# The order of the work in the first pair of sequences: copies, weight splits, finishes and sums change places

## The reference

```python
w1, w2 = W1[language_ids], W2[language_ids]              # layer 0: an adapter, 512 -> 128 -> 512
h = relu(x @ w1 + b1[language_ids])
y = x + h @ w2 + b2[language_ids]
x = x + layernorm(y) * gamma[language_ids] + beta[language_ids]
h = gelu(x @ W1m + b1m)                                  # layer 1: 512 -> 2048, shared weights
x = x + concat([h @ W2m + b2m,                           # 384 shared output columns
                h @ We[indices] + be[indices]], -1)      # 128 columns of the sequence's own expert
```

## Time and profile before

| | |
|---|---|
| median of 3 runs | 1474.71 us (1471.84 to 1479.5) |
| profiled execution | 1473.23 us, its span 1471.4 us |
| PE busy | 1449.9 us (99%) |
| DVE, POOL, ACT busy | 939.9, 649.4, 524.6 us |
| mean granted TensorE clock | 0.996 |

### The profile page before, as it was taken

How to read it: one execution, slowest core, us unless ns; L and a number is a source line. 1 busy time by engine, 2 the same in 40 slices (tenths; PEclk the granted TensorE clock), 3 DMA queues, 4 the chain that set the end, 5 groups by cost and what they waited for, 6 DMA issues and landing times.

```text
span 1471.4 us, 19128 instructions
## 1 busy us (share of the span) xinstructions
PE 1449.9 (99%) x6454; PEld 1189.2 (81%) x6454; DVE 939.9 (64%) x1597; ACT 524.6 (36%) x855; POOL 649.4 (44%) x639
## 2 busy tenths in 40 slices
PE   8989999999999999999999999999999999999999
PEld 5777778888887888888888888888888888888887
DVE  6878775766648666576566775666755776554444
ACT  4724353332533225322344322523234332342231
POOL 4795544623445334545246351483413843242101
PEclk9999999999999999999999999999999999999999
DMA  6655558444655536655356554456446464354332
GB/s 212 209 170 185 216 194 294 157 150 168 211 204 175 167 128 236 220 162 196 126 173 222 173 188 147 174 209 204 144 157 225 148 215 154 113 214 145 140 109 87
DMA packets 126617, 261.98 MB, mean 178 GB/s; under 512 B 11573, under 2 KB 83765, under 8 KB 118457
## 3 DMA queue, kind: packets, MB, share of 16 engines
q1 hardware_dynamic: 116724, 156.68, 33.3%
q10 hardware_dynamic: 9796, 104.08, 18.1%
HBM read 222.98 MB, written 37.75 MB: 177 GB/s over the span
## 4 chain that ended last, share of the span: by engine, by line
PE 90%; DVE 4%; POOL 3%; issue 2%; ACT 1%; ACTq 1%; DVEq 0%; POOLq 0%
PE down L251 15%; PE down L253 15%; PE down L252 15%; PE up_b L251 5%; PE up_b L253 5%; PE up_b L252 5%; PE up_c L251 4%; PE up_c L252 3%; PE up_c L253 3%; PE up_a L252 3%; PE up_a L253 3%; PE up_a L251 3%; DVE g L872 1%; PE aux L251 1%; PE aux L253 1%
## 5 line engine op out<-in xcount | busy, mean ns | idle before, releaser
L251 PE MATMUL down<-w,g 128*128 128x512 f32 x1024 | 401.6, 392 | 0.9 <-issue 0.5
L253 PE MATMUL down<-w,g 128*128 128x512 f32 x1024 | 398.9, 390 | 0.0
L252 PE MATMUL down<-w,g 128*128 128x512 f32 x1024 | 398.9, 390 | 0.0
L1198 POOL TENSOR_TENSOR w<-w_raw,ones 128x256 fp32r<-128x256 f32 x128 | 90.2, 704 | 633.9 <-DMA w_raw<-m_we 633.8
L251 PEld LDWEIGHTS down<-w,g 128*128 128x128 f32 x1024 | 192.5, 188 | 42.1 <-DVE g L872 1.9
L253 PEld LDWEIGHTS down<-w,g 128*128 128x128 f32 x1024 | 192.5, 188 | 40.5
L252 PEld LDWEIGHTS down<-w,g 128*128 128x128 f32 x1024 | 192.6, 188 | 39.4
L872 DVE TENSOR_TENSOR g<-g_raw,g 128x512 fp32r<-128x512 f32 x256 | 205.3, 818 | 22.9 <-ACT g L660 20.6
L658 ACT ACTIVATE g_raw<-up_a,m_b_sb 128x512 f32<-128x512 f32 x64 | 44.2, 690 | 413.7 <-PE up_a L253 386.0
L867 DVE TENSOR_TENSOR g_raw<-up_b,s 128x512 f32<-128x512 f32 x63 | 43.5, 691 | 225.0 <-PE up_b L253 180.9
L660 ACT CAST g<-g_raw 128x512 fp32r<-128x512 f32 x256 | 159.1, 621 | 8.1
(11 more groups left out here) (246 smaller groups left out, 2508.6 us busy)
## 6 DMA issues: line engine op xcount, KB each, us to landing
w<-w_kept ACTq DMA_DIRECT2D x55, 1792.0 KB, 7.6
w<-w_kept SPq DMA_DIRECT2D x56, 768.0 KB, 4.9
w_raw<-m_we SPq DMA_DIRECT2D x128, 128.0 KB, 4.6
out<-resid SPq DMA_DIRECT2D x64, 256.0 KB, 4.5
xTs_raw<-xT SPq DMA_DIRECT2D x56, 256.0 KB, 3.1
xs<-x SPq DMA_DIRECT2D x56, 256.0 KB, 4.6
w_kept<-w SPq DMA_DIRECT2D x8, 1792.0 KB, 8.0
aw_raw<-a_w SPq DMA_DIRECT2D x30, 256.0 KB, 4.5
```

Of the source, the lines that this page charges most:

```text
L251: eng.matmul(bank, a_hi, b_hi, start=opens, stop=False, skip_group_check=True)
L252: eng.matmul(bank, a_hi, b_lo, start=False, stop=False, skip_group_check=True)
L253: return eng.matmul(bank, a_lo, b_hi, start=False, stop=closes, skip_group_check=True)
L1198: eng.tensor_tensor(hi, values, ones[:, :, :].to_broadcast([P, 2, PART]), ALU.mult).then_inc(pool_eh[b], 1)
```

## The change

Only the order of instructions in the first pair and the split of one weight operation change. No product and no transfer is added or removed.

```diff
 pe_p1, second pair, k == 0:
-            eng.wait_ge(act_w1hi, GROUPS)
+            eng.wait_ge(pool_w1, 4)
             eng.wait_ge(dve_w1, GROUPS)
 act_second_step:
         act_g(eng, i, 1, C11)
-        act_w1_hi(eng, 2)
-        act_t_hi(eng, i, T4, 0)
-        act_t_hi(eng, i, T4, 1)
         act_xT_hi(eng, m, 0, 2)
         act_xT_hi(eng, m, 0, 3)
         act_aw_hi(eng, m, 0, 1)
+        act_t_hi(eng, i, T4, 0)
+        act_t_hi(eng, i, T4, 1)
         act_g(eng, i, 1, C12)
+        act_w1_hi(eng, 2)
         act_g(eng, i, 1, C22)
 act_step, last group, next pair's T1:
-            act_t_hi(eng, m, T1, 1)
-        act_g(eng, i, k, C22)
+            if i is not first:
+                act_t_hi(eng, m, T1, 1)
+        act_g(eng, i, k, C22)
+        if i is first and k == GROUPS - 1:
+            act_t_hi(eng, m, T1, 1)
 new:
+    def dve_finishes(eng, m, k):
+        if m and k - 1 in ADAPTER_DOWN:
+            b, t = ADAPTER_DOWN[k - 1]
+            dve_finish(eng, m, b, t)
+            dve_finish(eng, m, b, t + 1)
-    def dve_second_w1_lo(eng):
+    def dve_rest_w1_lo(eng, k):
+        eng.wait_ge(act_w1hi, k)
+        eng.tensor_tensor(w1[:, k % 2, LO, A22:7, :], w1_raw[:, k % 2, LO, A22:7, :], raw(w1[:, k % 2, HI, A22:7, :]),
                           ALU.subtract).then_inc(dve_w1, 1)
 dve_second_step:
         dve_sum_c22(eng, i, 1)
+        dve_xT_lo(eng, m, 0, 2)
+        dve_xT_lo(eng, m, 0, 3)
         dve_g_lo(eng, i, 0, C12)
         dve_g_lo(eng, i, 0, C22)
         dve_w2_lo(eng, 1)
         dve_g_lo(eng, i, 1, C11)
-        dve_xT_lo(eng, m, 0, 2)
-        dve_xT_lo(eng, m, 0, 3)
         dve_w1_lo(eng, 2)
 dve_step:
         elif i is not first:
-            dve_sum_c21(eng, before(i), GROUPS - 1)
+            if before(i) is not first:
+                dve_sum_c21(eng, before(i), GROUPS - 1)
...
             dve_sum_u2(eng, i, k)
-        if m and k - 1 in ADAPTER_DOWN:
-            (the two dve_finish)
+        if i is not first:
+            dve_finishes(eng, m, k)
...
         dve_sum_c22(eng, i, k)
         dve_g_lo(eng, i, k, C11)
+        if i is first:
+            dve_finishes(eng, m, k)
         (the two dve_add_adapter)
-        if i is first:
+        if i is first and k < GROUPS - 1:
             dve_w1_lo(eng, k + 1)
+        if i is first and k == GROUPS - 1:
+            dve_rest_w1_lo(eng, GROUPS)
+            dve_g_lo(eng, i, k, C12)
...
         if k == GROUPS - 1:
-            dve_g_lo(eng, i, k, C12)
+            if i is first:
+                dve_sum_c21(eng, i, k)
+            else:
+                dve_g_lo(eng, i, k, C12)
             dve_g_lo(eng, i, k, C22)
 pool_first_w1_lo: n == 3 does w1 slot 0, columns A11 to S4 (768), after act_w1hi 8
 pool_first_step:
-        if k == 2:
-            pool_aw_lo(eng, m, 1, 0)
         pool_weight_sums(eng, k + 1)
         if k == 1: (T4 low parts, experts, aw, the four pool_residual of sequence 0)
+            pool_aw_lo(eng, m, 1, 0)
         if k == GROUPS - 1:
-            for of, c in t_order(m)[:4]:
+            for n, (of, c) in enumerate(t_order(m)[:4]):
                 pool_t_lo(eng, m, of, c)
+                if n == 0:
+                    pool_first_w1_lo(eng, 3)
 start, PE: B21's first transpose goes right behind B11's two; each low pass of B21 behind its own
            transpose; C21 = A21 x B11 behind the B22 transposes
 start, ACT:
-            act_w1_hi(eng, 1)
+            act_first_part(eng, B11, 0, FIRST_B11[0])
             act_first_x_copy(eng, 3)
-            (first parts of B11, both c)
+            act_first_part(eng, B11, 1, FIRST_B11[1])
+            act_first_part(eng, B21, 0, FIRST_B21[0])
             (low parts of B11, both c)
-            (first parts of B21, both c)
+            act_w1_hi(eng, 1)
+            act_first_part(eng, B21, 1, FIRST_B21[1])
             (low parts of B21, both c)
```

More of the change, by code:

```diff
@@ L999, in dve_first_t4 @@
         eng.tensor_tensor(bo_raw[:, T4, c, LO, :], b21_raw(c), t2_raw(c), ALU.subtract).then_inc(dve_t, 1)
-    def dve_second_w1_lo(eng):
-        eng.wait_ge(act_w1hi, 1)
-        eng.tensor_tensor(w1[:, 1, LO, A22:7, :], w1_raw[:, 1, LO, A22:7, :], raw(w1[:, 1, HI, A22:7, :]),
+    def dve_rest_w1_lo(eng, k):
+        eng.wait_ge(act_w1hi, k)
+        eng.tensor_tensor(w1[:, k % 2, LO, A22:7, :], w1_raw[:, k % 2, LO, A22:7, :], raw(w1[:, k % 2, HI, A22:7, :]),
                           ALU.subtract).then_inc(dve_w1, 1)
@@ L1110, in dve_step @@
             dve_sum_u2(eng, i, k)
-        if m and k - 1 in ADAPTER_DOWN:
-            b, t = ADAPTER_DOWN[k - 1]
-            dve_finish(eng, m, b, t)
-            dve_finish(eng, m, b, t + 1)
+        if i is not first:
+            dve_finishes(eng, m, k)
         if m and k == 1:
@@ L1175, in pool_first_w1_lo @@
         else:
-            slot, s = 1, slice(A11, A22)
-            eng.wait_ge(act_w1hi, 1)
+            slot, s = 3 - n, slice(A11, A22)
+            eng.wait_ge(act_w1hi, 1 if n == 2 else GROUPS)
         eng.tensor_tensor(w1[:, slot, LO, s, :], w1_raw[:, slot, LO, s, :], raw(w1[:, slot, HI, s, :]),
@@ L1388, in keep_w1 @@
         eng.wait_ge(dve_w1, k)
-        if k == 1:
-            eng.wait_ge(pool_w1, 3)
+        if k in (1, GROUPS):
+            eng.wait_ge(pool_w1, 3 if k == 1 else 4)
         eng.dma_start(raw(w1_kept[k % GROUPS, :, :, :, :]), raw(w1[:, k % 2, :, :, :])).then_inc(kept_w1[k % 2], 16)
@@ L1573, in _ @@
                         pe_first_transpose(eng, B11, c, FIRST_B11[c])
+                    pe_first_transpose(eng, B21, 0, FIRST_B21[0])
                 if t == 2:
@@ L1576, in _ @@
                         pe_first_low(eng, B11, c, FIRST_B11[c])
-            pe_first_transpose(eng, B21, 0, FIRST_B21[0])
             pe_first_b12(eng, 0)
@@ L1580, in _ @@
             pe_first_transpose(eng, B21, 1, FIRST_B21[1])
+            pe_first_low(eng, B21, 0, FIRST_B21[0])
             eng.wait_ge(pool_w1, 2)
@@ L1583, in _ @@
             pe_first_b12(eng, 1)
-            for c in range(2):
-                pe_first_low(eng, B21, c, FIRST_B21[c])
+            pe_first_low(eng, B21, 1, FIRST_B21[1])
             pe_first_b12(eng, 2)
-            first_half(eng, C21, A21, B11, True, False)
             pe_first_b12(eng, 3)
@@ L1590, in _ @@
                 pe_transpose(eng, first, 1, 2 + c, FIRST_B22[c])
+            first_half(eng, C21, A21, B11, True, False)
             eng.wait_ge(b_low, 4)
@@ L1624, in _ @@
                 act_first_x_copy(eng, t)
-            act_w1_hi(eng, 1)
+            act_first_part(eng, B11, 0, FIRST_B11[0])
             act_first_x_copy(eng, 3)
-            for c in range(2):
-                act_first_part(eng, B11, c, FIRST_B11[c])
+            act_first_part(eng, B11, 1, FIRST_B11[1])
+            act_first_part(eng, B21, 0, FIRST_B21[0])
             for c in range(2):
                 act_first_low(eng, B11, c, FIRST_B11[c])
-            for c in range(2):
-                act_first_part(eng, B21, c, FIRST_B21[c])
+            act_w1_hi(eng, 1)
+            act_first_part(eng, B21, 1, FIRST_B21[1])
             for c in range(2):
@@ L1677, in _ @@
                 dve_b_lo(eng, first, B22, c, FIRST_B22[c])
-            dve_second_w1_lo(eng)
+            dve_rest_w1_lo(eng, 1)
             for c in range(2):
```

## The result

The changed kernel took 1468.88 us (median of 20 runs, 1464.7 to 1473.86), the kernel before 1473.43 us on the same chip (20 runs, 1471.16 to 1479.5). The ratio is 0.9973, with a 95% interval of 0.9965 to 0.9981: 4.0 us faster (2.8 to 5.2). The forecast was 8.4 us. The profiled execution took 1472.54 us, only 0.7 us less than the one of before (1473.23), and is one of the slowest of the 20.

A forecast was written before the change was run, and what follows sets the result against it. PE is busy 99% of the span, so only its first-pair gaps and the slow clock behind them can be won. Group 3's 3.4, groups 4 and 5's 2.3 and the boundary's 2.7 make 8.4 us: 1465.5 us, range 1459 to 1471.5.

The forecast's parts named there:

- The start: Before group 1: B11's first part ahead of ACT's weight cast brings PE to group 1 0.5 us sooner.
- Group 1: xT's 1.82 us wait goes, but PE waits about 2.8 us for DVE's w1 low part of group 2.
- The adapter's wait: Group 2: POOL has aw's low part ready at 77, PE wants it at 82; the 4.14 us wait goes.
- Group 3's down product: Sequence 0 in group 3: expert weights split at 119.9, a new wait of about 2.4 us, net gain 3.4 us.
- (b): Rival: DVE and POOL, sharing SBUF, mostly eat the savings; 4.5 us gained, 1470 us; chance 0.20.
- Groups 4 and 5: First pair: C12 ahead of the finishes removes the waits of 1.29 and 1.00 us, 2.3 us gained.
- The boundary: End of first pair: gap 1.6 instead of 3.0 us, gain 1.8, clock 0.9, together 2.7 us (0 to 4.8).
- the likeliest case: The forecast itself, 8.4 us faster over the whole kernel, own range 1462 to 1468.5 us; chance 0.52.
- the outcomes that had 0.37: Whole kernel: time within about 0.5% (7.4 us) of the kernel before, not told from no change; chance 0.37.
- the 0.59: Whole kernel: faster by more than one measurement's 7.4 us, below the line at 1467.3 us; chance 0.59.
- (a): Rival: all PE gaps close, expert weights in time; 14.1 us gained, 1460 us; chance 0.20.
- (c): Rival: xT lands late, SP's chain delays group 3's experts; 1.6 us slower, 1476 us; chance 0.08.

The follow-up runs named there:

- e1: Changed kernel with group 3's kept w2, raw w2 and expert weights issued on SP ahead of the next pair's biases and x loads: 1468.09 us, 0.9967.
- e3: Changed kernel with group 3's two finishes alone put back ahead of the sum C12: 1466.03 us, 0.9942 of the kernel before.
- e8: Kernel before with only the first pair's two finishes moved behind C12, C22 and C11's low part: 1470.55 us, 0.998.
- e9: The changed kernel again without any edit, run for a second profile: 1469.76 us, 0.9968 of the kernel before.
- e2: Changed kernel with SP's store of group 4's split W1 held until POOL has split group 3's expert weights: 1470.86 us, 0.998.
- e6: e5 with POOL's weight sums for group 3 ahead of the biases and of sequence 1's expert of group 1: 1471.80 us, 0.9993.
- e5: Changed kernel with the edits of e1 and e4, and DVE's w2 low part of group 3 ahead of the adapter's moments: 1467.11 us, 0.9959.
- e4: Changed kernel with DVE's low part of group 2's W1 two places earlier: 1471.17 us, 0.9979 of the kernel before.
- e10: Changed kernel with the edits of e3 and e4 together: 1465.74 us, 0.9943 of the kernel before.
- e7: Kernel before with only POOL's low part of sequence 1's first adapter weights moved behind group 1's residuals: 1469.53 us, 0.9981.
- e11: Changed kernel with its edits at the end of the first pair undone (old boundary): 1469.97 us, 0.998 of the kernel before.
- e12: Kernel before with only the change's new order of ACT and DVE in group 1: 1470.69 us, 0.9977.

## Why the prediction was right in direction and half right in size

**The start, -0.5 us. Right.** #0 itself moved by 5 us over the profiles, but that scatter lies ahead of PE's first `up_b<-bo,ones_row`, a matmul of the start at 22.9 to 27.5 us. From there to #0 it is 32.8 us in all four profiles with the old start and 32.4 in all ten with the new one, so the new start gives 0.4 us. The line before (#0 at 56.83), then after (#0 at 56.20):

```profile
24.00 0.47 PE L500 MATMUL up_b<-bo,ones_row 64*128 64x512 f32 x1 [0.33 <-ACT x L696]
...
23.82 0.46 PE L500 MATMUL up_b<-bo,ones_row 64*128 64x512 f32 x1 [0.33 <-ACT x L696]
```

**Group 1: the saving is moved, not made. Right.** ACT's xT at 56.4 (57.0 expected), POOL's T4 at 58.75 (58.8), DVE's w1 low part done at 68.85 (68.2), PE's wait there 3.5 us (2.8), 1.2 GHz behind it, sequence 0's down product at 72.2 (71; 72.35 before). The subtraction of 1792 columns cost what it did before; it is the two low parts of g ahead of it that went from 1.45 to 2.81 us once POOL ran beside them. The Trainium skill (GPSIMD Engine Reference, "Key points") says that the two engines contend for their shared SBUF interfaces when VectorE has two SBUF inputs; the row agrees. Together with w2's low part and the next g's, the four small subtractions went from 3.1 to 6.1 us, 0.75 each, where the forecast's upper bound had half a us each for five.

**The adapter's wait. Right.** `aw` was ready at 78.0 (77), the 4.14 us and their clock are gone.

**Group 3's down product: the term that failed.** The forecast put it at 119.9, "PE's gain there is 124.74 - 119.9 = 4.8 us", net of clock 3.4. It began at 123.86 and 123.15: a gain of 0.9 and 1.6 us. Three of its inputs were off (and a fourth reading, that DVE has nearly no idle time from 44 to 112 us, doesn't fit the trace of before, where DVE stands idle 6.2 us up to 91.25; the chain below doesn't use it):

- *The head of the chain.* POOL's list from T4 to the sums for group 3 took 29.6 us against 28.2 before: sums done at 88.3 instead of 86.9. DVE's subtraction behind ACT's cast took 2.74 us where 2.07 was carried over from the earlier trace rows. It ended at 92.8, 2.1 us after the 90.7 of the forecast, and the 19.0 us from there to the end of the finishes were right (18.8): 111.7 instead of 109.7. DVE kept 2.1 of the 4.2 us. That fits rival (b)'s mechanism: POOL kept 2.1 of its 3.4 where (b) had 1.5.
- *Its tail.* From the finishes' end to the end of the split, 10.2 us of queue and landing were copied from one profile of before. They were 12.1 in the first profile (experts landed after 6.8 us instead of 4.9) and 10.7 in the second. The tail was ended by POOL's expert split, as forecast, though the list names DVE's low part of w2, which was done 0.6 us sooner. In the first profile the split was done at 123.76, against 123.75 before: nothing of the whole chain's gain was left there. e1 shows the chain's cause by taking it away, e3 by starting it earlier.
- *The clock behind it* was charged with 1.4 us. #5 to #6 without a gap is 12.24 us (e3); it took 15.20 and 13.78: 3.0 and 1.5 us.

Net, the term was 0.9 - 3.0 = -2.1 us in one execution and 1.6 - 1.5 = 0.1 in the other, where 3.4 was forecast.

**Groups 4 and 5, 2.3 us. Right.** No C12 wait in the first pair's groups 4 and 5 in any variant with the late finishes there; e8 measures 2.3.

**The boundary, 2.7 us. Nearly right.** C21's wait went, the last is 1.6 us (1.6). #12 to #13, where 1.8 us were forecast, gave 1.2 (14.75 to 13.58). The rest is a small wait that the forecast didn't have, in every execution with the new boundary:

```profile
217.88 0.47 PE L251 MATMUL down<-w,g 128*128 128x512 f32 x1 [0.57 <-issue]
```

POOL's expert split for it, the row at 216.57, ended 0.10 us before. POOL now has the 768-column piece ahead of it (2.83 us beside DVE, where 1.85 were forecast); before, that split ended at 217.42, 1.9 us before PE came. For the clock the forecast said that it is kept in half of the cases: with the 1.6 us wait, the stretch between #13 and #14 was 10.96 to 11.00 us in four executions (e9, e1, e2, e6; also in e5, which has no such wait) and 12.4 to 12.6 in four (the first profile, e3, e4, e10). With the old one it was 11.97 to 13.50 in all five (before, e7, e8, e11, e12). Mean #12 to #14: old 27.4, new 25.4 without e5 (which has no wait there), so 2.0 us. By time, e11 against e9 doesn't show it (0.2 us); the interval of each is wider than the forecast 1.2 to 2 us, so the gain rests on the stretches alone.

**The sum.** Up to #14, 0.8 us in the first profile and 4.6 in the second, the start counted in; the median says 4.5, the ratio 4.0. The forecast was 8.4. Nearly all that is missing is in group 3's term; the other terms came to 2.9 and 4.5 us where 5.0 was forecast. For the same reason #12 came only 0.3 and 2.5 us early, where the forecast had pair 2 beginning 5 to 7 us early. 1468.9 us is inside the range but just outside the likeliest case's own (1462 to 1468.5), and above 1467.3, the prediction's own line for a change that one measurement can tell: it falls among the outcomes that had 0.37, not among the 0.59. What was gained is about what C12 (2.3) and the boundary (2.0) gave; the term that was to bring most brought nothing. In the first profile, with group 3's wait at 4.75 us, 0.8 us were left up to #14; that most executions seem to fare better (2.7 to 3.4 us in the four other profiles with that wait) is, for the prediction, luck.

**Why parts don't add.** By medians, group 1's order alone gave 2.8 us (e12), `aw` alone 3.0 (e7) and the finishes alone 2.0 (e8), 7.9 together, without the boundary; all of them in one kernel gave 4.0. The intervals of the three are 1.5 to 2.4 us wide to each side, so by time this difference only just shows. The first two take the same 4.14 us wait from two sides (0.8 us of it is left in e12, none in e7), so they can't both be paid for it; and in the whole kernel PE, ahead by then, stands for the queue behind the finishes, as e1 and e3 show.

**Rivals.** (a) needed the expert weights in time: PE stood at 119.1 us and they were split at 123.76. (b) was priced at 1470 with exactly this contention; the measured 1468.9 lies between it and the forecast. (c) needed xT late: it landed as its row said. What the runs leave open is why the same loads land after 5.3 us in one execution and 7.5 in another (raw w2), 4.6 and 6.8 (experts).

## What to carry to other kernels

When an edit moves an engine's early work forward, follow it to the next place where a queue must run through a fixed delay (an issue order, a DMA, a cast, a split), and compare its end with the other engines' new time, not the old: e3 gave up 1.4 us of a short wait and won 3.5. Copy a delay that contains DMAs from several executions or give it a range of its own, since one profile's 6.1 us was 7.5 in another of the same kernel. Check a releaser's name against the clock: put its end beside the waiter's start, and beside the ends of the other things that the instruction waits for. A gap of PE has a second price that isn't in the list of waits, and one profile shows only one draw of it: compare stretches between landmarks of at least two.

## What was not expected of the hardware

- The clock behind equal gaps isn't equal. At the boundary a 1.6 us wait was followed by a granted clock of 0.66 and 0.50 in one execution and 1.00 in another. Behind 4.14 us the slow matmuls cost 1.7 us, behind 4.75 us 3.0, behind 2.7 us 1.5.
- Pairs 2 to 8, the same instructions in all kernels, took 1217.4 to 1224.7 us. The longest (e3's profile) has two waits for C12 there, 1.7 and 1.2 us, the second longest (e1's) one of 1.6, the others none above 1 us; this hides a gain of 5 us in a single execution. e3's median of 6 runs was the lowest but one all the same.
- Over the 20 runs of the changed kernel the time goes with the mean granted clock (correlation -0.75): 1473.86 us at 0.992, 1464.7 at 0.999. Much of the spread of 9 us goes so with the clock; whether the clock or the gaps behind which it falls come first, the times don't show.
- A DVE subtraction with two inputs in SBUF is 0.6 to 0.7 us for 512 columns when POOL is idle and was up to 2.3 us beside it (below, in the profile after, beside POOL's 768-column piece); one of 1792 columns took 2.0 to 3.1.

```profile
206.71 2.34 DVE L875 TENSOR_TENSOR g<-g_raw,g 128x512 fp32r<-128x512 f32 x1
```
